# Down weight pieces moved among the steps of a fused attention and feed-forward kernel

## The reference

```
xn  = layernorm(x)
att = softmax(causal(q k^T / sqrt(512))) v o_proj + xn      # q, k, v from layernorm(xn)*gamma+beta
h   = silu(xn @ w_gate) * (xn @ w_up)                       # 512 -> 2048
h   = keep the 2 largest |h| of every 4, zero the others
out = x + att + h @ w_down                                  # 2048 -> 512
```

## Time and profile before

| | |
|---|---|
| median of 3 runs | 797.4 us (796.82, 797.4, 801.81) |
| profiled execution | 800.95 us, span 799.2 us from first to last instruction |
| PE busy | 785.4 us, 98% of the span, 3734 matmuls |
| PEld busy | 658.5 us, 82% |
| DVE busy | 630.1 us, 79% |
| ACT busy | 365.4 us, 46% |
| POOL busy | 62.9 us, 8% |
| mean granted clock of TensorE | 0.994 of full speed |
| HBM traffic | 191 GB/s over the span |

### The profile page before, as it was taken

The page is one execution under the profiler, slowest core; times in us unless marked ns, Lnnn a source line. Parts: engine busy times, 40 slices in busy tenths (PEclk is TensorE's granted clock), DMA queues, the critical chain, the costliest instruction groups (busy, mean ns, idle before and its releaser), DMA issues.

```text
span 799.2 us, 9954 instructions
## 1 busy us (share of the span) xinstructions
PE 785.4 (98%) x3734; PEld 658.5 (82%) x3734; DVE 630.1 (79%) x998; ACT 365.4 (46%) x600; POOL 62.9 (8%) x70
## 2 busy tenths in 40 slices
PE   9999999999997999999999999999999999999998
PEld 7888888878886887788887888888898898898887
DVE  6979788688753698779989788699778669669786
ACT  5423351235222364554547537355554464465541
POOL 2011110010010000010100010100101100100100
PEclk9999999999999999999999999999999999999999
DMA  9441705511244438486747869599757767665602
GB/s 321 180 160 59 233 0 208 181 71 54 107 155 160 155 131 309 144 321 251 249 104 258 321 134 358 137 422 325 227 221 234 214 248 230 181 231 112 157 2 106
DMA packets 40240, 153.26 MB, mean 192 GB/s; under 512 B 3648, under 2 KB 4224, under 8 KB 36992
## 3 DMA queue, kind: packets, MB, share of 16 engines
q1 hardware_dynamic: 28080, 122.66, 40.3%
q0 software_dynamic: 10816, 27.79, 15.4%
q10 hardware_dynamic: 1296, 2.16, 0.8%
HBM read 85.99 MB, written 66.62 MB: 191 GB/s over the span
## 4 chain that ended last, share of the span: by engine, by line
PE 65%; DMA 2%; ACT 1%; DVE 1%; issue 1%; SPq 0%; DVEq 0%; ACTq 0%
PE bank L1094 12%; PE bank L1095 12%; PE bank L1096 12%; PE bank L1177 4%; PE bank L1179 4%; PE bank L1178 4%; PE bank L1210 3%; PE bank L1212 3%; PE bank L1211 3%; PE bank L832 2%; PE bank L834 2%; PE bank L833 2%; DMA X_raw<-block_sums 1%; DMA wsum<-w_units 1%; DMA result<-rows 1%
## 5 line engine op out<-in xcount | busy, mean ns | idle before, releaser
L1094 PE MATMUL bank<-X_hi,wset 128*128 128x512 f32 x448 | 175.6, 392 | 4.0 <-ACT bank L1409 3.0
L1096 PE MATMUL bank<-X_hi,wset 128*128 128x512 f32 x448 | 175.1, 391 | 0.0
L1095 PE MATMUL bank<-X_lo,wset 128*128 128x512 f32 x448 | 175.0, 391 | 0.0
L1094 PEld LDWEIGHTS bank<-X_hi,wset 128*128 128x128 f32 x448 | 84.5, 189 | 23.3 <-ACT bank L1409 4.2
L1096 PEld LDWEIGHTS bank<-X_hi,wset 128*128 128x128 f32 x448 | 84.5, 189 | 17.8
L1095 PEld LDWEIGHTS bank<-X_lo,wset 128*128 128x128 f32 x448 | 84.5, 189 | 17.0
L825 POOL DMA_DIRECT2D result<-staged x26 | 31.5, 1213 | 333.0 <-ACT staged L1482 116.9
L832 PE MATMUL bank<-zg,xT 128*128 128x512 f32 (+2 forms) x132 | 50.6, 383 | 4.2 <-ACT wide_raw L1388 4.2
L834 PE MATMUL bank<-zg,xT 128*128 128x512 f32 (+2 forms) x132 | 49.9, 378 | 0.0
L833 PE MATMUL bank<-zg,xT 128*128 128x512 f32 (+2 forms) x132 | 49.9, 378 | 0.0
L1177 PE MATMUL bank<-dw,hs_hi 128*128 128x512 f32 x128 | 49.9, 389 | 0.0
(11 more groups left out here) (294 smaller groups left out, 1746.5 us busy)
## 6 DMA issues: line engine op xcount, KB each, us to landing
w_operands<-wset SPq DMA_DIRECT2D x8, 3584.0 KB, 13.5
wset<-w_operands SPq DMA_DIRECT2D x8, 3584.0 KB, 12.1
result<-staged POOLq DMA_DIRECT2D x26, 512.0 KB, 5.5
down_operands<-prep POOLq DMA_DIRECT2D x6, 1792.0 KB, 8.5
wsum<-w_units SPq DMA_DIRECT2D x28, 256.0 KB, 4.0
dwop<-down_operands SPq DMA_DIRECT2D x3, 2048.0 KB, 11.4
dwop<-down_operands SPq DMA_DIRECT2D x3, 1536.0 KB, 11.9
xw<-L_attn_x SPq DMA_DIRECT2D x4, 1024.0 KB, 9.9
```

The source lines that it names most:

```text
L1094: pe.matmul(dst[:], u[:, 0, :], x_hi, start=(first and kt == 0), stop=False, skip_group_check=True)
L1095: pe.matmul(dst[:], u[:, 0, :], x_lo, start=False, stop=False, skip_group_check=True)
L1096: last = pe.matmul(dst[:], u[:, 1, :], x_hi, start=False, stop=(kt == 1), skip_group_check=True)
```

## The change

Pieces 0 to 3 of the down weight get other places in `steps`; pieces 4 and 5 other places in the loops over n; POOL's loads of pieces 0 and 4 get one more wait each; and the row sums of chunk 3 come ahead of the low half of the last input.

```
 in steps, chunk 2:
-  *u[2:4], xn[2][0], *prep_sum[0], *u[4:6], *prep_hi_steps[0], xn[2][1], ...
+  *u[2:4], xn[2][0], *u[4:6], xn[2][1], ...
-  xh[3][3], *prep_lo[0], prep_store[0], prep_load[1], *z_round[3], *z[3][0:2]
+  xh[3][3], *prep_sum[0], *prep_hi_steps[0], *z_round[3], *z[3][0:2]
-  softmax(2, {-1: [z[3][2]], ...}, {3: prep_sum[1], 4: [*prep_hi_steps[1], xn[3][0]], ...})
+  softmax(2, {-1: [prep_lo[0][0], z[3][2]], ...},
+          {1: [prep_lo[0][1], prep_store[0], prep_load[1]], 4: [xn[3][0]], ...})
-  *prep_lo[1], prep_store[1], prep_load[2], ("sum_turn", 2, 0), ...
+  *prep_sum[1], *prep_hi_steps[1], *prep_lo[1], prep_store[1], prep_load[2], ("sum_turn", 2, 0), ...
 chunk 3:
-  *u[0:2], *prep_sum[2], u[2], *prep_hi_steps[2], u[3], *rows_of[2][2], ..., *rows_of[2][3], ...,
-  *prep_lo[2], prep_store[2], prep_load[3], *u[4:6], ("w_sum", 0, 0), u[6], ...
+  *u[0:4], *rows_of[2][2], ..., *rows_of[2][3], ..., *prep_sum[2], *u[4:6], *prep_hi_steps[2],
+  *prep_lo[2], prep_store[2], prep_load[3], ("w_sum", 0, 0), u[6], ...
-  *X_lo_steps[4:], ("sum_turn", 3, 0), *rows_of[3][0], ...
+  *X_lo_steps[4:6], ("sum_turn", 3, 0), X_lo_steps[6], *rows_of[3][0], ...
 load_prep (POOL):
   if p == 0:
       ...
+      pool.wait_ge(rows_ready, OLD + TC)
+  if p == PREP_FIRST:
+      pool.wait_ge(T_loaded[T4], 16)
 ACT, loop over n:
+  after up_seed(n):            if n == 1: prep_operands_hi(PREP_FIRST, 0); (PREP_FIRST, 1)
-  after the third Silu:        if n == 0: prep_operands_hi(PREP_FIRST, 0); (PREP_FIRST, 1)
   for t in range(TC):
       keep_down(i, t)
+      if n == 3 and t < 2:
+          prep_operands_hi(PREP_LATE, t)
-  if n == 3: prep_operands_hi(PREP_LATE, 0); (PREP_LATE, 1)        # behind the four copies
 DVE, loop over n:
+  ahead of first_hidden(n):    if n == 1: prep_operands_lo(PREP_FIRST, 0); (PREP_FIRST, 1)
-  ahead of last_block(n):      if n == 0: prep_sums(PREP_FIRST, 0); (PREP_FIRST, 1)
   after last_block(n), n == 0:
-      prep_operands_lo(PREP_FIRST, 0); (PREP_FIRST, 1)
+      prep_sums(PREP_FIRST, 0); (PREP_FIRST, 1)
```

More of the change, by code:

```diff
@@ L140, in attention_ffn @@
     steps += [*u[0:2], *rows_of[1][2], *rows_of[1][3], ("rows_load", OLD + 4, 0), ("rows_load", OLD + 5, 0), *u[2:4], xn[2][0],
[L141 to L145, removed]
+              *u[4:6], xn[2][1], xn_store[2], u[6], xh_pre[3][0], u[7], xh_pre[3][1], xh[3][0], u[8], xh_pre[3][2], xh[3][1], u[9],
+              xh_pre[3][3], xh[3][2], *u[10:], ("max_fold", 2, 0), ("max_all", 2, 0), xh[3][3], *prep_sum[0], *prep_hi_steps[0], *z_round[3], *z[3][0:2]]
+    steps += softmax(2, {-1: [prep_lo[0][0], z[3][2]], 0: [z[3][3]], 1: v[2][0:2], 2: v[2][2:4]},
+                     {1: [prep_lo[0][1], prep_store[0], prep_load[1]], 4: [xn[3][0]], 5: [xn[3][1], xn_store[3]]})
+    steps += [*prep_sum[1], *prep_hi_steps[1], *prep_lo[1], prep_store[1], prep_load[2], ("sum_turn", 2, 0), *rows_of[2][0], ("rows_load", OLD + 6, 0), *rows_of[2][1],
               ("rows_load", OLD + 7, 0)]
@@ L151, in attention_ffn @@
     w_hi_steps, w_lo_steps = fills("w_hi", 0), fills("w_lo", 0)
-    steps += [*u[0:2], *prep_sum[2], u[2], *prep_hi_steps[2], u[3], *rows_of[2][2], ("rows_load", OLD + 8, 0), *rows_of[2][3], ("rows_load", OLD + 9, 0),
-              *prep_lo[2], prep_store[2], prep_load[3], *u[4:6], ("w_sum", 0, 0), u[6], *w_hi_steps[0:2], *u[7:9], *w_lo_steps[0:2], *u[9:], ("max_fold", 3, 0),
+    steps += [*u[0:4], *rows_of[2][2], ("rows_load", OLD + 8, 0), *rows_of[2][3], ("rows_load", OLD + 9, 0), *prep_sum[2], *u[4:6], *prep_hi_steps[2],
+              *prep_lo[2], prep_store[2], prep_load[3], ("w_sum", 0, 0), u[6], *w_hi_steps[0:2], *u[7:9], *w_lo_steps[0:2], *u[9:], ("max_fold", 3, 0),
               ("max_all", 3, 0), ("X_load", 0, 0), v[3][0], v_keep[0], *v[3][1:4]]
@@ L158, in attention_ffn @@
                       6: [X_lo_steps[0], v_keep[3], X_hi_steps[1], X_hi_steps[2]], 7: [X_lo_steps[1], X_hi_steps[3], X_hi_steps[4]]})
-    steps += [("T4_load", 0, 0), *X_lo_steps[2:4], *X_hi_steps[5:], *X_lo_steps[4:], ("sum_turn", 3, 0), *rows_of[3][0], *rows_of[3][1], *rows_of[3][2], *rows_of[3][3]]
+    steps += [("T4_load", 0, 0), *X_lo_steps[2:4], *X_hi_steps[5:], *X_lo_steps[4:6], ("sum_turn", 3, 0), X_lo_steps[6], *rows_of[3][0], *rows_of[3][1], *rows_of[3][2], *rows_of[3][3]]
     def key_tiles(i):
@@ L1498, in _ @@
                     up_seed(n)
+                if n == 1:
+                    prep_operands_hi(PREP_FIRST, 0)
+                    prep_operands_hi(PREP_FIRST, 1)
                 if n == N_Q - 1:
@@ L1550, in _ @@
                 nc.scalar.activation(g_sum[3][:], bank[0][:], ACT.Silu).then_inc(silu_ready, 1)
-                if n == 0:
-                    prep_operands_hi(PREP_FIRST, 0)
-                    prep_operands_hi(PREP_FIRST, 1)
                 if n == 1:
@@ L1590, in _ @@
                         keep_down(i, t)
-                    if n == 3:
-                        prep_operands_hi(PREP_LATE, 0)
-                        prep_operands_hi(PREP_LATE, 1)
+                        if n == 3 and t < 2:
+                            prep_operands_hi(PREP_LATE, t)
             act.wait_ge(full[1], FILLS * N_Q)
@@ L2044, in _ @@
                     last_beats(i)
+                if n == 1:
+                    prep_operands_lo(PREP_FIRST, 0)
+                    prep_operands_lo(PREP_FIRST, 1)
                 first_hidden(n)
@@ L2104, in _ @@
                 nc.vector.tensor_tensor(b_tile(n, 0)[:], g_sum[3][:], bank[1][:], ALU.mult).then_inc(hid_ready, 1)
-                if n == 0:
-                    prep_sums(PREP_FIRST, 0)
-                    prep_sums(PREP_FIRST, 1)
                 if i in BLOCKED:
@@ L2112, in _ @@
                 if n == 0:
-                    prep_operands_lo(PREP_FIRST, 0)
-                    prep_operands_lo(PREP_FIRST, 1)
+                    prep_sums(PREP_FIRST, 0)
+                    prep_sums(PREP_FIRST, 1)
                 elif n == 3:
```

## The result

| | before | changed |
|---|---|---|
| median | 798.67 us (796.82 to 801.81, 4 runs) | 786.22 us (784.92 to 787.5, 4 runs) |
| profiled execution | 800.95 us, span 799.2 | 784.92 us, span 783.1 |
| ratio | | 0.984, 95% interval 0.9801 to 0.9879 |

The forecast was 787.3 us, with a range of 784.5 to 792.3. The kernel is 1.6% faster, and the two profiled executions differ by 16.0 us.

What follows compares the result with a forecast made beforehand. PE, busy 785.4 of 799.2 us, was taken as the bound. Gains of 14.2 us, less three allowances of 0.2, made 13.6: from the profiled 800.95 to 787.3 us, range 784.5 to 792.3.

Steps and rivals of the forecast that it cites:

- The loss and its floor: Whole kernel: 10.1 us of PE waits plus 5.0 of half clock can be won, nothing below 785.8 us.
- Chunk 2's scores, 3.6: PE's 1.9 us wait for score copies and the 1.7 of half clock behind it go.
- Chunk 2's softmax, 0.2: Piece 0's sums, copies and lows moved here delay z and cost 0.2 us of PE wait.
- the margin that I had read: Chunk 2's values: a low half is ready 2.1 us before PE takes it, against 2.2 of added delay.
- Chunk 3's scores, 4.9: w_units loads issued 2.4 us earlier cut PE's 4.2 us wait to 1.0; the 1.7 of half clock goes.
- the bounds for the landing: Chunk 3's w_units loads: landing unchanged leaves PE a 1.8 us wait, shorter landing leaves none; 1.0 was taken.
- list of signs: What would show the prediction right, among it w_units issued near 3 us earlier against PE's first score product of chunk 3.
- Row sums, 1.0: Chunk 3: the reduction put ahead of the last input's low half removes PE's 1.0 us wait.
- groups, 3.5 and 1.2: PE's seed copy waits go: group 0 to 1 gains 3.5 us with its half clock, group 3 to 4 1.2.
- The slower rival: Chunk 3: jammed stores of rows 8 to 11 make w_units 12.4 us later; 804.6 us, chance 0.04.
- list of what would show it wrong: PE waits in chunk 2 for wide_lo or row sums, or stores of rows 8 to 11 landing later than 4.2 us.

Runs made afterwards that it cites:

- groups' kernel: The kernel before with pieces 4 and 5 at new places in groups 0, 1 and 3, and POOL's wait ahead of piece 4's load; 793.67 us, ratio 0.9928.
- chunk 2 alone: The kernel before with only pieces 0 and 1 moved and POOL's load of piece 0 waiting for row 7; 800.51 us, ratio 1.0012.

## Why the prediction was right, and which steps were off

*The loss and its floor.* I read 10.1 us of waits and 5.0 of half clock, floor 785.8. The profile gave back 16.0 and stands 0.9 under that floor. PE's idle time fell by 10.0 us (from 799.2 - 785.4 to 783.1 - 779.3), which is the sum of waits. Its busy time fell by 6.1, 1.1 more than I had for the half clocks. So the surplus is in busy time and not in further gaps; which matmuls gave it I did not find out.

*Profile against median.* The profiled execution of before was among its heavier ones, with mean clock 0.994; other runs of it show 0.998 to 0.994, as much as one to three stretches of 3.4 us. I worked from the floor and not from the median minus 13.6, and that held: the changed kernel's four runs show no half clock and lie within 2.6 us. The gain by medians is 12.5, by profiles 16.0. Against the medians the terms also made up for each other, which is luck: chunk 2's 3.6 was too much, chunk 3's term 2.2 and the groups' 1.1 too little, as said below.

*Chunk 2's scores, 3.6.* The chain came 2.3 us earlier (2.5 predicted) and the wait went. About 1.5 us of this are the four subtractions that left, as predicted; 0.85 is an earlier start of DVE (145.79 for 146.64), where I had 1. But that this earlier start comes from POOL's held loads is not shown, since the stores landed in 4.2 us without the wait. And the term was too large for the median: this wait was 0.3 to 1.9 in five executions of the same code and reached a half clock in two. Beside the other parts it is worth about 0.

*Chunk 2's softmax, 0.2.* z was late enough for 0.3 of PE; the margin that I had read kept 1.26 where I had reckoned none, because DVE's pauses for ACT took up the low. Right in size, too dark in the working.

*Chunk 3's scores, 4.9.* Issue moved from 22.6 to 20.4 us behind the chunk's first score product, 2.2 earlier (2.4 predicted). The value I took between the bounds for the landing, a wait of 1.0, was too cautious: being first gave the short landing. Alone the part measured 7.1. It is the largest term and the one with the least margin left, 0.5 us. The list of signs has the w_units "near 3 us" earlier where the sum has 2.4; 2.2 bears out the sum.

*Row sums, 1.0; groups, 3.5 and 1.2.* The row sums' wait went, as did those of the groups. The groups' kernel won 6.8 by medians where I had 4.7, but its 6.8 hold the row sums' 1.0 too, so it is to be set against 5.7. I had put that 1.0 down to the new order; POOL's wait, which the prediction gives no price, does it alone in the trace of the groups' kernel.

*The slower rival.* Row stores 8 to 11 did land later, 3.6 at the median and 4.8 at most in place of 2.6 and 4.2. Stores later than 4.2 stood on the prediction's list of what would show it wrong, so that sign appeared. But SP's waits for them grew only from 9.4 to 12.5 us in all. Most of it is the store of row 8, the first, and fell into DVE's pause of 8.08 us. The mechanism is there, at almost no price while that pause lasts. It is not what took chunk 2's gain away in the kernel with that part alone: there SP issued the loads behind the stores of rows 10 and 11 2.0 and 3.1 us after them, where it was 2.0 and 3.0 before, and the delay was DVE's wait for piece 2's load.

## What to carry to other kernels

When an engine is 98% busy, sum its waits and its stretches at half clock before judging a change: here they gave the gain within a microsecond. They are cured by moving work that nobody waits for out of the chain that someone waits for. Take a transfer that must be early ahead of a large store that need not be; here 1.5 us in the issue, from just ahead of the store to just behind it, cost three in the landing. A part that moves work later should be tried together with the part that makes room for it, since alone it may only move the wait.

## What the runs showed of the hardware

A VectorE subtraction of 128x256 that takes 0.42 us took 1.26 at 169.22, while POOL's all-reduce over partitions ran from 168.75 to 170.94; the next three took 0.41 to 0.42, the first of them from 170.40 on, still inside that stretch. That the all-reduce is the cause is not shown. A half clock lasted 3.4, 6.8 or, behind the longest wait (6.8 us, chunk 2 alone), 10.2 us, part of it while PE still stands. The landing of the same two row stores, issued at the same place, ranged from 3.5 to 6.6 us between the thirteen profiled executions.
